# A selective state-space mixer on one core: six of sixteen input terms by diagonal products, a ring of four state buffers, wider products and scans

## What is computed

```python
def step(state, xs):
    d_t, B_t, C_t, u_t = xs
    dA = jnp.exp(d_t[..., None] * A)
    state = state * dA + (d_t * u_t)[..., None] * B_t[:, None, :]
    y_t = jnp.einsum('ben,bn->be', state, C_t)
    return (state, y_t)
```

## Time and profile before

| | us |
|---|---|
| median of 3 runs | 697.18 (697.15 to 697.28) |
| the profiled execution's own time | 699.17 |
| its span, first to last instruction | 697.4 |
| busy in the span: ACT, PE, DVE, POOL | 565.9, 553.5, 548.0, 490.5 |
| state stage | 155.38 to 493.69 |

### The profile page before, as it was taken

One profiled execution on the slowest core, in us unless ns is written; L12 is line 12 of the kernel. 1 busy time (PEld: TensorE's weight loads), 2 busy tenths in 40 slices (PEclk: granted clock), 3 DMA queues, 4 the chain that ended last, 5 costly groups with the idle time before them and its releaser, 6 DMA issues.

```text
span 697.4 us, 10143 instructions
## 1 busy us (share of the span) xinstructions
PE 553.5 (79%) x3560; PEld 391.0 (56%) x3560; DVE 548.0 (79%) x815; ACT 565.9 (81%) x769; POOL 490.5 (70%) x253
## 2 busy tenths in 40 slices
PE   5877788116897778877897776868889999999975
PEld 2433335116786768776786776866345454545442
DVE  3972262548999999999999999999499898988761
ACT  3873636759999999999999997977378898989773
POOL 2999255006999989999999986889455656555561
PEclk9988657557999999999999998899899999999999
DMA  8900090930121136221722228121300000000000
GB/s 281 361 1 0 0 344 25 382 129 31 48 60 54 53 84 189 61 62 57 207 72 60 59 53 267 47 56 37 60 1 16 31 26 22 30 16 31 16 31 30
DMA packets 25076, 59.16 MB, mean 85 GB/s; under 512 B 5105, under 2 KB 5105, under 8 KB 23362
## 3 DMA queue, kind: packets, MB, share of 16 engines
q1 hardware_dynamic: 22914, 54.32, 22.9%
q0 software_dynamic: 2112, 4.19, 3.5%
HBM read 47.89 MB, written 10.62 MB: 84 GB/s over the span
## 4 chain that ended last, share of the span: by engine, by line
ACT 44%; PE 36%; DVE 8%; POOL 5%; issue 4%; DMA 3%; POOLq 0%; DVEq 0%; SPq 0%; ACTq 0%
ACT arena L506 19%; ACT arena L510 19%; PE ps L942 15%; PE ps L957 6%; ACT arena L453 3%; PE ps L797 3%; PE ps L779 3%; PE ps L885 2%; DVE arena L640 2%; DVE arena L571 2%; POOL arena L321 2%; PE ps L896 2%; PE ps L949 2%; DMA arena<-w_all 1%; DMA arena<-ctx_t 1%
## 5 line engine op out<-in xcount | busy, mean ns | idle before, releaser
L354 POOL TENSOR_TENSOR arena<-arena 128x1024 f32<-128x1024 f32 x128 | 300.4, 2388 | 68.1 <-DVE arena L640 55.4
L640 DVE TENSOR_TENSOR_SCAN arena<-arena,ps 128x512 f32<-128x512 f32 x256 | 290.2, 1199 | 22.1 <-PE ps L885 16.6
L885 PE MATMUL ps<-ident,arena 128*128 128x128 f32 x1024 | 161.8, 283 | 76.0 <-ACT arena L506 63.0
L885 PEld LDWEIGHTS ps<-ident,arena 128*128 128x128 f32 x1024 | 121.3, 145 | 91.0 <-ACT arena L506 68.5
L506 ACT ACTIVATE arena<-arena,bT 128x512 f32<-128x512 f32 x256 | 162.9, 706 | 4.7 <-DMA w_ternary<-arena 4.7
L896 PE MATMUL ps<-ident,arena 128*128 128x128 f32 x1024 | 158.9, 278 | 8.1 <-DVE arena L647 4.7
L510 ACT ACTIVATE arena<-arena,a_neg 128x512 f32<-128x512 f32 x256 | 163.2, 707 | 0.1
L896 PEld LDWEIGHTS ps<-ident,arena 128*128 128x128 f32 x1024 | 123.0, 143 | 11.1 <-POOL arena L354 4.8
L942 PE MATMUL ps<-arena 128*128 128x512 bf16 x512 | 120.9, 386 | 4.8 <-DVE arena L724 2.6
L382 POOL TENSOR_TENSOR arena<-arena 128x1024 f32<-128x1024 f32 x32 | 75.4, 2355 | 26.6 <-DVE arena L724 26.6
L942 PEld LDWEIGHTS ps<-arena 128*128 128x128 bf16 x512 | 49.3, 99 | 61.0 <-issue 8.6
(11 more groups left out here) (90 smaller groups left out, 641.7 us busy)
## 6 DMA issues: line engine op xcount, KB each, us to landing
arena<-c_rows SPq DMA_DIRECT2D x64, 256.0 KB, 3.2
arena<-w_all SPq DMA_DIRECT2D x12, 1024.0 KB, 9.5
w_ternary<-arena SPq DMA_DIRECT2D x12, 512.0 KB, 7.7
arena<-w_ternary SPq DMA_DIRECT2D x3, 2048.0 KB, 10.1
arena<-x SPq DMA_DIRECT2D x4, 1024.0 KB, 8.1
arena<-x POOLq DMA_DIRECT2D x4, 1024.0 KB, 12.4
out<-arena SPq DMA_DIRECT2D x16, 256.0 KB, 2.0
arena<-ctx_t SPq DMA_DIRECT2D x2, 1024.0 KB, 8.5
```

The source lines that it names most:

```text
L354: nc.gpsimd.tensor_tensor(ps_[:, s, 2 * half:2 * half + 2, :], hs[:, s, 2 * half:2 * half + 2, :], c_bc[:, s:s + 1, :].to_broadcast([P, 2, ...
L640: nc.vector.tensor_tensor_scan(out=hs[:, s, i, :], data0=dA[:, s, i, :], data1=ps[:, 4 + i, :], initial=0.0, op0=ALU.mult, op1=ALU.add).th ...
L885: last = nc.tensor.transpose(ps[:, 4 + i, c * P:(c + 1) * P], dB[:, s, c, i * P:(i + 1) * P], ident[:])
```

## The change

- **Input term.** For the states n of DIAG = (1, 3, 9, 11, 13, 15), ACT no longer scales `turned`. It scales the 128x128 identity by B into `dgB` (two slots), four activations of 128x128, and PE makes the input term by true float32 products `turned` x `dgB`, four for each `turn(k, i)`, in place of four transposes. For the other ten states `dB` stays, but with one buffer in place of two (`turned_before`: ACT waits until PE has turned the last state that used the buffer).
- **Buffers.** `hs` is a ring of four; `ps_` is gone. POOL's product is one instruction of 128x2048 written in place, with one increment of `p_ready` for a state. PE's `add` waits for that one.
- **Scans.** Two scans of 128x1024 for a state in place of four of 128x512. Column 0 of every `dA` block is set to zero once (DVE, strided, before the first scan), which restarts the recurrence at a block's border; the exponentials leave it out (511 columns). `scan_done` counts two for a state.
- The order of PE's loop, `add_skip`, the gate, the loads and the feed-forward block stay.

```diff
+RING = 4
+DIAG = (1, 3, 9, 11, 13, 15)
-        dB = part(112, 16).rearrange("p (s k e) -> p s k e", s=2, k=KL)
-        hs = part(128, 16).rearrange("p (s k l) -> p s k l", s=2, k=KE)
-        ps_ = part(144, 16).rearrange("p (s k l) -> p s k l", s=2, k=KE)
+        dB = part(112, 8).rearrange("p (k e) -> p k e", k=KL)
+        dgB = part(120, 4).rearrange("p (s k e) -> p s k e", s=2, k=KL)
+        hs = part(128, 32).rearrange("p (s k l) -> p s k l", s=RING, k=KE)
...
+        def is_diag(k):
+            return k % DS in DIAG
+        def diag_slot(k):
+            return (k // DS * len(DIAG) + DIAG.index(k % DS)) % 2
+        def turned_before(k):
+            same = [j for j in range(k) if is_diag(j) == is_diag(k) and (not is_diag(k) or diag_slot(j) == diag_slot(k))]
+            return same[-1] * KE + KE if same else 0
...
-                hold(sp, "p_ready", (k - 2) * 2 + 2)
+                hold(sp, "p_ready", k - 1)
...
-                for half in range(2):
-                    hold(pool, "scan_done", k * KE + 2 * half + 2, *added(k - 2, half))
-                    nc.gpsimd.tensor_tensor(
-                        ps_[:, s, 2 * half:2 * half + 2, :], hs[:, s, 2 * half:2 * half + 2, :],
-                        c_bc[:, s:s + 1, :].to_broadcast([P, 2, L]), ALU.mult).then_inc(S["p_ready"], 1)
+                pool.wait_ge(S["scan_done"], k * 2 + 2)
+                nc.gpsimd.tensor_tensor(hs[:, k % RING, :, :], hs[:, k % RING, :, :],
+                                        c_bc[:, s:s + 1, :].to_broadcast([P, KE, L]),
+                                        ALU.mult).then_inc(S["p_ready"], 1)
...
-                    hold(act, "dBu_ready", (k - 2) * KE + KE)
+                    hold(act, "dBu_ready", turned_before(k))
                     for i in range(KL):
-                        nc.scalar.activation(dB[:, s, i, :], turned[:, b, i, :], ACT.Copy,
-                                             scale=bT[:, b, i, n:n + 1]).then_inc(S["dB_ready"], 1)
+                        if is_diag(k):
+                            nc.scalar.activation(dgB[:, diag_slot(k), i, :], ident[:], ACT.Copy,
+                                                 scale=bT[:, b, i, n:n + 1]).then_inc(S["dB_ready"], 1)
+                        else:
+                            nc.scalar.activation(dB[:, i, :], turned[:, b, i, :], ACT.Copy,
+                                                 scale=bT[:, b, i, n:n + 1]).then_inc(S["dB_ready"], 1)
                     for i in range(KE):
-                        hold(act, "scan_done", (k - 2) * KE + i + 1)
-                        nc.scalar.activation(dA[:, s, i, :], delta_u[:, b, 0, i, :], ACT.Exp,
+                        hold(act, "scan_done", (k - 2) * 2 + i // 2 + 1)
+                        nc.scalar.activation(dA[:, s, i, 1:], delta_u[:, b, 0, i, 1:], ACT.Exp,
                                              scale=a_neg[:, i, n:n + 1]).then_inc(S["dA_ready"], 1)
...
             def scan(k):
-                b, s = k // DS, k % 2
-                for i in range(KE):
-                    hold(dve, "p_ready", (k - 2) * 2 + i // 2 + 1)
-                    dve.wait_ge(S["dA_ready"], k * KE + i + 1)
-                    dve.wait_ge(S["dBu_ready"], k * KE + i + 1)
-                    nc.vector.tensor_tensor_scan(out=hs[:, s, i, :], data0=dA[:, s, i, :], data1=ps[:, 4 + i, :],
-                                                 initial=0.0, op0=ALU.mult, op1=ALU.add).then_inc(S["scan_done"], 1)
+                for h in range(2):
+                    two = slice(2 * h, 2 * h + 2)
+                    if k >= RING:
+                        hold(dve, *added(k - RING, h))
+                    dve.wait_ge(S["dA_ready"], k * KE + 2 * h + 2)
+                    dve.wait_ge(S["dBu_ready"], k * KE + 2 * h + 2)
+                    nc.vector.tensor_tensor_scan(out=flat(hs[:, k % RING, two, :]), data0=flat(dA[:, k % 2, two, :]),
+                                                 data1=flat(ps[:, 4 + 2 * h:6 + 2 * h, :]), initial=0.0, op0=ALU.mult,
+                                                 op1=ALU.add).then_inc(S["scan_done"], 1)
...
+            for k in range(4):
+                dve.wait_ge(wq_stored[k], 16 * 3)
+            step(nc.vector.memset(dA[:, :, :, 0], 0.0))
...
             def turn(k, i):
-                s = k % 2
                 pe.wait_ge(S["dB_ready"], k * KL + KL)
-                hold(pe, "scan_done", (k - 1) * KE + i + 1)
+                hold(pe, "scan_done", (k - 1) * 2 + i // 2 + 1)
                 for c in range(KL):
-                    last = nc.tensor.transpose(ps[:, 4 + i, c * P:(c + 1) * P], dB[:, s, c, i * P:(i + 1) * P],
-                                               ident[:])
+                    to = ps[:, 4 + i, c * P:(c + 1) * P]
+                    if is_diag(k):
+                        last = mm(to, turned[:, k // DS, c, i * P:(i + 1) * P], dgB[:, diag_slot(k), c, :], start=True,
+                                  stop=True)
+                    else:
+                        last = nc.tensor.transpose(to, dB[:, c, i * P:(i + 1) * P], ident[:])
                 last.then_inc(S["dBu_ready"], 1)
...
-                pe.wait_ge(S["p_ready"], k * 2 + i // 2 + 1)
+                pe.wait_ge(S["p_ready"], k + 1)
...
-                    last = mm(ps[:, c, i * P:(i + 1) * P], ps_[:, s, i, c * P:(c + 1) * P], ident[:],
+                    last = mm(ps[:, c, i * P:(i + 1) * P], hs[:, k % RING, i, c * P:(c + 1) * P], ident[:],
```

More of the change, by code:

```diff
@@ L880, in turn @@
             def turn(k, i):
-                s = k % 2
                 pe.wait_ge(S["dB_ready"], k * KL + KL)
-                hold(pe, "scan_done", (k - 1) * KE + i + 1)
+                hold(pe, "scan_done", (k - 1) * 2 + i // 2 + 1)
                 for c in range(KL):
-                    last = nc.tensor.transpose(ps[:, 4 + i, c * P:(c + 1) * P], dB[:, s, c, i * P:(i + 1) * P],
-                                               ident[:])
+                    to = ps[:, 4 + i, c * P:(c + 1) * P]
[4 more added lines that the diff above has]
+                        last = nc.tensor.transpose(to, dB[:, c, i * P:(i + 1) * P], ident[:])
                 last.then_inc(S["dBu_ready"], 1)
             def add(k, i):
-                b, n, s = k // DS, k % DS, k % 2
-                pe.wait_ge(S["p_ready"], k * 2 + i // 2 + 1)
+                b, n = k // DS, k % DS
+                pe.wait_ge(S["p_ready"], k + 1)
                 for c in range(KL):
@@ L926, in turn_q1 @@
                 last.then_inc(S["q1T_psum"], 1)
-            pe.wait_ge(S["scan_done"], NB * DS * KE)
+            pe.wait_ge(S["scan_done"], NB * DS * 2)
             turn_q1(0)
```

## The result

The change made the kernel slower: 778.08 us (776.85 to 779.60, 4 runs) against 697.23 (697.15 to 698.66, 4 runs), a ratio of 1.1155 with a 95% interval of 1.113 to 1.118. The forecast was 757 us in a range of 733 to 790, with 0.90 for slower: the time lies in the range, 21 us above the forecast.

What follows compares the result with a forecast made beforehand. ACT was taken to bound the kernel before, and loops of waits the changed one. The stage's terms came to 546, 52 behind 493.7; with 8 for the clock, 60 on the 697.4 span, giving a forecast of 757 us, range 733 to 790.

Steps and rivals of the forecast that it cites:

- Busy time: State stage: by busy time alone ACT 4.4, DVE 4.45, POOL 4.50, PE 4.4 us, 0.4 us less a state.
- rival A: State stage: PE's order is covered and POOL at 4.50 us sets the pace; faster, 673 us; chance 8%.
- The product loop: PE's turns of k+2 queue behind adds awaiting whole product k: 10.31 us for two states, 11.22 with a diagonal one.
- 2 for the gate: Between batches: gate_y on DVE is no longer in slack, 2 us each in three batches, 6 in all.
- The buffer loop: Plain states after plain ones: ACT waits for PE's last turn from the one dB; 5.93 us, 6.6 with add_skip.
- True products: PE's diagonal turns: four true float32 products at 0.22 us each, 0.88 us a turn, 1.05 to its last end.
- Rival B: PE's diagonal turns: true products in a row take 0.44 us each, a pair of states 13.8; 820 us; chance 8%.
- The clock: PE's pauses of 2.4 us in plain states after plain ones lower its clock: 8 us taken, bounds nothing and 27.
- The normalisation in the last batch: Some 5 us on DVE three times, against 2.3 us of slack in a pair of states: 4 us added.
- The rule's upper end of 13 us: Last batch's three normalisations: DVE instructions may wait for POOL's running product, up to 4.5 us each, where 4 was taken.
- From the execution to the median: Whole kernel: the median shown is 2.0 us below the profiled execution, so 759 became 757 us.
- Rival C: State stage: half the one-dB wait is hidden and the clock stays; 733 us, down to 700; chance 10%.

Runs made afterwards that it cites:

- turns-first run: The changed kernel with PE's order alone edited: all four turns of state k+2, then all four adds of state k; 712.36 us, ratio 1.020 to the kernel before.

## Why the prediction was right, and where it was off

- **Busy time was not the bound.** Right: the prediction set the sums by engine (4.4 to 4.5 us a state) aside, rival A with them, because the waits had changed and PE's order had not. The turns-first run shows it from the other side.
- **The product loop.** Right in each link. 11.38 us measured for 11.22: the whole product is 0.06 longer, and a PE group that starts after a wait takes 0.49 us to the next instead of 0.44. But the sum gave six such pairs to a batch, and only the states 10 to 15 run at that pace, 2 us over twelve pairs. The states 8 and 9 take 10.6 us together, which takes the 2 us back. The pair behind a gate takes 14.9, 15.4 and 14.8 us where 13.2 were put (11.22 and 2 for the gate): 5 us of the miss. So a part of the pairs' agreement is luck.
- **The buffer loop.** Right: 6.6 us, and 16 us come back with two buffers. The four steps of a batch take 26.8, 28.6 and 26.9 us in the first three batches where 25.7 were put, and 25.3 with PE kept busy, so what is above goes with the clock.
- **True products.** Right: 0.89 us for four, so 0.22 each also in a row. Rival B, and the rule beside it in "TensorE: Matmul & The Clock Gate" of the Trainium skill (Terms, a transpose four times faster for float32), don't hold here: 0.89 against 0.44 is twice.
- **The clock.** Right in kind; 10 us by experiment where 8 were taken. The falls behind the gates were not foreseen; they are in the 5 us above.
- **The normalisation in the last batch: the step that failed.** The prediction put 4 us for it. From the first scan of state 33 to that of state 47 the kernel after takes 444.62 - 357.99 = 86.6 us, and from state 49 to 63, the same states with the normalisation, 558.70 - 456.00 = 102.7. The difference is 16 us, so the term was mis-sized. The rows of DVE, with the chain behind state 51 between them:

```profile
357.99 2.29 DVE L657 TENSOR_TENSOR_SCAN arena<-arena,ps 128x1024 f32<-128x1024 f32 x1 [2.08 <-PE ps L907]
...
444.62 2.29 DVE L657 TENSOR_TENSOR_SCAN arena<-arena,ps 128x1024 f32<-128x1024 f32 x1 [2.08 <-PE ps L907]
...
456.00 2.29 DVE L657 TENSOR_TENSOR_SCAN arena<-arena,ps 128x1024 f32<-128x1024 f32 x1 [1.09 <-PE ps L907]
...
475.22 0.66 DVE L697 TENSOR_REDUCE am<-arena 128x1 f32<-128x512 f32 x1
...
480.89 4.45 DVE L657 TENSOR_TENSOR_SCAN arena<-arena,ps 128x1024 f32<-128x1024 f32 x2
...
558.70 4.59 DVE L657 TENSOR_TENSOR_SCAN arena<-arena,ps 128x1024 f32<-128x1024 f32 x2 [2.42 <-PE ps L920]
```

The kernel before had shown the size. Its third batch, from the first scan of state 32 to that of state 48, takes 78.5 us, and its last, to the end of state 63's scans at 487.17, takes 92.9:

```profile
315.77 4.55 DVE L640 TENSOR_TENSOR_SCAN arena<-arena,ps 128x512 f32<-128x512 f32 x4 [0.35 <-PE ps L885]
...
394.26 4.55 DVE L640 TENSOR_TENSOR_SCAN arena<-arena,ps 128x512 f32<-128x512 f32 x4 [0.35 <-PE ps L885]
...
469.29 17.88 DVE L640 TENSOR_TENSOR_SCAN arena<-arena,ps 128x512 f32<-128x512 f32 x16
```

So the normalisation cost 14 us before and 16 after. It is little of why the kernel after is slower, but a sum that builds the stage from its start has to carry it whole, and this one carried 4 of it. The term's working set a chain of some 5 us against 2.3 us of DVE's slack in a pair; but that slack lies ahead of the first scan of the odd states (the 2.07 us in the timeline above), and the long part of the chain stands between an odd state and the even one behind it, where three scans run without a pause. So nothing hid it: from the chain's first instruction to the next scan it takes 5.67, 5.48 and 5.43 us, 16.6 together. Waiting for the running product is 9.2 us of them (L729 at 3.5 us three times instead of 0.48), since one scan releases both the chain and the product; before, with shorter products, the same chain took 3.66, 5.13 and 3.65. The rule's upper end of 13 us was near the 16, but the waits it spoke of are those 9.2.
- **From the execution to the median.** 2.0 us were taken off, since the profiled execution of the kernel before was that much above its median; the one of the kernel after (778.36) is 0.3 above its own.

The sum was therefore 60 us on the span, where 79 were measured: 12 of the missing 19 are the normalisation, 5 the pairs behind the gates and 2 the clock. With the 2 us of the last point that makes the 21. The parts are read in different ways (the clock's from a run, the others from the trace), so each is good to about 1 us. Rival C's gain in the buffer loop didn't occur.

## What to carry to other kernels

When an edit makes a producer's unit larger (one product of 2048 for two of 1024) while a consumer engine keeps a hand-written order, walk that order once and ask what stands behind each wait: here turns queued between the adds of a whole product cost 66 us, in both loops together, and moving a loop header gave them back. When a sum builds a stage from its start, check it first on the kernel before: here that would have shown the 14 us of the last batch. Balanced busy sums say what is possible, and only the loop of waits from a buffer's use to its next use says what happens. A buffer taken away to make room (dB) should be tried against the one given (the fourth hs, worth nothing here).

## What the runs showed of the hardware

- Some DVE instructions (L729, float32 to float32, and L731, float32 to bf16, both from SBUF to SBUF) wait for a running GpSimd product and end 0.28 to 0.29 us behind it at the places shown; shorter products don't help if the next one follows at once, because the next DVE instruction is caught in turn.
- True float32 products of 128x128 in a row run at 0.11 us a record, two records each, as a single one does.
- Transposes that nobody reads, in PE's pauses, made the kernel 10 us faster; the granted clock went from 0.94 to 0.98 in the middle window, and from 0.86 to 1.00 in the buffer loop's states.
